# Attention products as 64x32 tiles, with the order of the second pass's steps changed

## The reference, cut to what matters

```python
Q = query @ Wq + bq            # 32 query heads, 4 groups on each of 8 key/value heads, 16 wide
K = key @ Wk + bk
V = value @ Wv + bv
scores = einsum('bhgqd,bhkd->bhgqk', Q, K) * scale
w = softmax(scores, axis=-1)
y = einsum('bhgqk,bhkd->bhgqd', w, V)
x = x + y @ Wo + bo
...
logits = x_n @ gate_w;  routing_weights = top_k(logits, 2)
shared_out = (relu(x_n @ up_w) ** 2) @ down_w
routed_out = (x_n @ fc1_w @ expert_w * sum(routing_weights)) @ fc2_w
x = x + layernorm(shared_out + routed_out, gamma, beta)
```

## Time and profile before

| what | us |
|---|---|
| median of 3 runs (685.68 to 687.26) | 686.53 |
| the profiled execution | 687.42 |
| its span in the profile | 685.6 |
| second pass from its turn -1 to the end | 245.7 to 685.6 |

### The profile page before, as it was taken

How to read it: one execution, slowest core, us unless ns; L and a number is a source line. 1 busy time by engine, 2 the same in 40 slices (tenths; PEclk the granted TensorE clock), 3 DMA queues, 4 the chain that set the end, 5 groups by cost and what they waited for, 6 DMA issues and landing times.

```text
span 685.6 us, 12653 instructions
## 1 busy us (share of the span) xinstructions
PE 654.6 (95%) x3964; PEld 482.3 (70%) x3964; DVE 511.4 (75%) x1140; ACT 432.0 (63%) x793; POOL 378.5 (55%) x464
## 2 busy tenths in 40 slices
PE   7889999999999898999999999999999999998986
PEld 3455666666656476788778787887878878786775
DVE  4999998999975877777677677776777767775444
ACT  4788888888746785574655846658367474674221
POOL 1388999888775534435455354554454545535351
PEclk9999999999999999999999999999999999999999
DMA  8334434352126321121212312113021221211000
GB/s 269 121 109 124 139 123 124 123 180 98 62 94 173 117 79 33 46 64 61 63 35 57 90 33 61 45 49 90 31 61 54 69 61 31 61 31 47 17 16 31
DMA packets 32551, 54.37 MB, mean 79 GB/s; under 512 B 5344, under 2 KB 7136, under 8 KB 32512
## 3 DMA queue, kind: packets, MB, share of 16 engines
q1 hardware_dynamic: 32512, 53.90, 26.6%
HBM read 36.84 MB, written 8.39 MB: 66 GB/s over the span
## 4 chain that ended last, share of the span: by engine, by line
PE 78%; DVE 11%; issue 4%; DMA 3%; ACT 3%; POOL 1%; SPq 0%; POOLq 0%; DVEq 0%; ACTq 0%
PE ps_b L1295 8%; PE ps_b L1297 7%; PE ps_b L1296 7%; PE wide L1295 7%; PE wide L1297 6%; PE wide L1296 6%; PE ps_b L1496 4%; PE ps_a L1340 4%; PE bank L1432 3%; DMA ctx_t<-in_ctx 3%; PE wide L1422 3%; PE ps_b L1350 3%; PE ps_a L1295 2%; PE ps_a L1297 2%; PE wide L1550 2%
## 5 line engine op out<-in xcount | busy, mean ns | idle before, releaser
L780 POOL TENSOR_TENSOR va<-mv,small 128x1 f32<-128x1 f32 x80 | 15.3, 192 | 149.0 <-DVE mv L1274 79.5
L745 ACT ACTIVATE stage<-wide 128x512 f32<-128x512 f32 x30 | 16.3, 595 | 83.8 <-PE bank L1597 83.7
L868 POOL TENSOR_TENSOR y_l<-y,y_h 128x512 fp32r<-128x512 f32 x16 | 21.9, 1370 | 72.5 <-ACT y_h L653 72.5
L1142 DVE RECIPROCAL y<-ps_b 128x256 f32<-128x256 f32 x32 | 55.9, 1748 | 0.4 <-PE ps_b L1496 0.4
L676 ACT ACTIVATE probs<-wide 128x1024 f32<-128x1024 f32 x32 | 32.8, 1025 | 36.1 <-PE wide L1550 36.1
L1295 PE MATMUL wide<-up_h,t_h 128*128 128x512 f32 x128 | 52.1, 407 | 1.5 <-DVE t_l L1226 1.5
L1297 PE MATMUL wide<-up_h,t_l 128*128 128x512 f32 x128 | 50.9, 398 | 0.0
L1296 PE MATMUL wide<-up_l,t_h 128*128 128x512 f32 x128 | 50.4, 394 | 0.0
L1295 PE MATMUL ps_b<-down_h,ht_h 128*128 128x512 f32 x120 | 49.6, 413 | 0.4 <-DVE ht_l L1214 0.4
L782 POOL TENSOR_TENSOR rs<-va,small 128x1 f32<-128x1 f32 x80 | 44.5, 557 | 6.3
L1297 PE MATMUL ps_b<-down_h,ht_l 128*128 128x512 f32 x120 | 47.2, 393 | 0.0
(11 more groups left out here) (244 smaller groups left out, 2155.9 us busy)
## 6 DMA issues: line engine op xcount, KB each, us to landing
q_stack<-qt_h SPq DMA_DIRECT2D x128, 64.0 KB, 2.0
ctx_t<-in_ctx SPq DMA_DIRECT2D x16, 256.0 KB, 2.7
x_res<-in_x SPq DMA_DIRECT2D x16, 256.0 KB, 2.9
x_in<-x_rows SPq DMA_DIRECT2D x16, 256.0 KB, 2.7
ctx_t<-in_ctx_turned SPq DMA_DIRECT2D x16, 256.0 KB, 2.9
x_res<-x_rows SPq DMA_DIRECT2D x16, 256.0 KB, 2.9
out<-stage SPq DMA_DIRECT2D x15, 256.0 KB, 3.0
x_in<-in_x SPq DMA_DIRECT2D x8, 256.0 KB, 3.0
```

The lines of the kernel that those rows point to most:

```text
L1142: dve.reciprocal(y[:, :, b, :], part[:, 1]).then_inc(S["den_s"], 1)
```

## The change

Tiles 0 and 1 keep the old products (`apart(t)`, `APART = 2`). From tile 2 on:

- `vbd` is filled with ones outside its diagonal blocks (once, at tile 2), so the tile of one head and one batch is 64 rows by 32 columns: 16 of values and 16 of ones. `attend` makes 16 products of 64x32 where it made 16 of 128x32: head h of a pair sits in rows 64h on and writes bank 2+h. The numerators of head 0 and the denominators of head 1 of a pair then stand in the wrong halves for each other: in bank 2 rows 0 to 15 of a pair's 32 are numerators and rows 16 to 31 denominators, in bank 3 it is the other way round.
- ACT copies both banks out (`attended_out`: two copies `sums`, then a third of bank 2, scaled by a 0/1 column into `y`). SP moves the denominators to their rows with eight DMAs of 16 rows (`denominators`), ahead of `stacked`. DVE adds the masked numerators of bank 3 (`numerators`), takes two reciprocals in SBUF (`inverted`) and multiplies once (`attended`).
- `output` does its eight products with `y_h` before it waits for `y_l`, then the four with `y_l`.
- Steps are moved on each engine. On PE: `turned_hidden(i, 0)` ahead of `turned_queries`; the routed upper half behind `down(i, 0)`; `output` behind `down(i, 1)`; `turned_norm` and `turned_maxima` behind `output`; both `scores` ahead of `queries`, with `products_kv` between them. On ACT: `y_high`, `query_high` and `guard_rows` follow one another behind `queries_stacked`; both `weights_of` ahead of the routed copies. On DVE and POOL as the diff shows.

```diff
-            def attend(t):
+            def attend_ready(t):
                 if live(t):
                     pe.wait_ge(S["vbd_s"], t + 1)
                     wait(pe, S["kv_s"], capped(1, t + 2))
                     wait(pe, S["z_s"], t - 2)
+                    pe.wait_ge(S["probs_s"], 2 * t + 2)
+            def attend(t):
+                if apart(t):
...
+                elif live(t):
+                    for b in range(2):
+                        for p in range(PAIRS):
+                            for h in range(2):
+                                k = slice(SEQ * h, SEQ * (h + 1))
+                                last = pe.matmul(bank[2 + h][STACK * p:STACK * (p + 1), HALF * b:HALF * (b + 1)],
+                                                 vbd[k, b, p].rearrange("k h d -> k (h d)"), probs[k, b, p, :],
+                                                 start=True, stop=True)
                         last.then_inc(S["pv_ps"], 1)
...
             def output(t):
                 if live(t):
+                    pe.wait_ge(S["y_hi"], t + 1)
+                    for g in range(GROUPS):
+                        pe.matmul(bank[2], cols(y_h, g, P), cols(wo_h, g, D), start=(g == 0), stop=False)
+                        pe.matmul(bank[2], cols(y_h, g, P), cols(wo_l, g, D), start=False, stop=False)
                     pe.wait_ge(S["y_lo"], t + 1)
                     for g in range(GROUPS):
-                        last = split_product(bank[2], cols(y_h, g, P), cols(y_l, g, P),
-                                             cols(wo_h, g, D), cols(wo_l, g, D), g == 0, g == GROUPS - 1)
+                        last = pe.matmul(bank[2], cols(y_l, g, P), cols(wo_h, g, D), start=False, stop=(g == GROUPS - 1))
                     last.then_inc(S["wo_ps"], 1)
...
+            def denominators(t):
+                if live(t) and not apart(t):
+                    sp.wait_ge(S["sums_s"], 2 * (t - APART) + 1)
+                    wait(sp, S["wo_ps"], t)
+                    for h in range(2):
+                        for p in range(PAIRS):
+                            at, beside = STACK * p + HD * h, STACK * p + HD * (1 - h)
+                            sp.dma_start(den[at:at + HD], sums[h][beside:beside + HD]).then_inc(S["den_in"], 16)
...
             def body2(i):
                 load2(i + 4)
-                stacked(i + 3)
                 residual(i + 2)
+                denominators(i + 2)
...
+                stacked(i + 3)
...
+            def attended_out(t):
+                if live(t) and not apart(t):
+                    act.wait_ge(S["pv_ps"], 2 * t + 2)
+                    act.wait_ge(S["qy_ps"], capped(1, t + 2))
+                    for h in range(2):
+                        last = act.activation(sums[h][:].rearrange("p g b q -> p b g q"),
+                                              bank[2 + h].rearrange("p (b g q) -> p b g q", b=2, g=GROUPS), ACT.Copy)
+                    last.then_inc(S["sums_s"], 1)
+                    wait(act, S["wo_ps"], t)
+                    act.activation(y[:].rearrange("p g b q -> p b g q"),
+                                   bank[2].rearrange("p (b g q) -> p b g q", b=2, g=GROUPS), ACT.Copy, scale=place[0]
+                                   ).then_inc(S["sums_s"], 1)
...
+                elif live(t):
+                    dve.wait_ge(S["sums_s"], 2 * (t - APART) + 2)
+                    dve.scalar_tensor_tensor(y[:], sums[1][:], place[1], y[:], ALU.mult, ALU.add).then_inc(S["den_s"], 1)
+            def inverted(t, b):
+                if live(t) and not apart(t):
+                    dve.wait_ge(S["den_in"], DEN_MOVES * (t - APART + 1))
+                    dve.reciprocal(den[:, :, b, :], den[:, :, b, :]).then_inc(S["den_s"], 1)
```

More of the change, by code:

```diff
@@ L157, in build @@
         x_in, ctx_t = sb("x_in", [P, D]), sb("ctx_t", [P, D])
+        with ExitStack() as tmp:
+            sums = [sb(f"sums{h}", [P, GROUPS, 2, SEQ], stack=tmp) for h in range(2)]
         x_h, x_l = sb("x_h", [P, D], F32R), sb("x_l", [P, D], F32R)
@@ L284, in build, with apart, folded @@
         LEAD2 = 4
+        APART = 2
+        def apart(t):
+            return isinstance(t, int) and t < APART
+        def folded(n, tiles):
+            return n * (min(max(tiles, 0), NT - APART) if isinstance(tiles, int) else tiles)
         MOVES = 16 * 2 * PAIRS
+        DEN_MOVES = 16 * 2 * PAIRS
         EARLY = NT - 2
@@ L750, in body2 @@
                     hidden_high(NT - 1, 0)
+                queries_stacked(i + 3)
+                y_high(i + 2)
+                query_high(i + 4)
                 if opening(i):
-                    guard_rows(2)
-                    query_high(3)
                     down_high(1)
-                else:
-                    query_high(i + 4)
-                    guard_rows(i + 3)
+                guard_rows(i + 3)
                 weights_of(i + 3, 0)
+                weights_of(i + 3, 1)
                 t = i + 1
@@ L1233, in body2 @@
                     hidden_low(t, 0)
+                keys_low(i + 3)
+                queries_low(i + 3)
+                numerators(i + 2)
+                context_low(i + 4)
+                normalised(i + 4)
+                maxima(i + 3, 0)
+                inverted(i + 2, 0)
+                t = i
+                if live(t) and not final(t):
+                    hidden_low(t, 1)
+                inverted(i + 2, 1)
                 attended(i + 2)
-                if opening(i):
-                    down_low(0)
+                maxima(i + 3, 1)
                 t = i + 1
@@ L1243, in body2 @@
                     dve.tensor_tensor(rw[:], lg[:, 0:1], lg[:, 1:2], ALU.add).then_inc(S["rw_s"], 1)
-                maxima(i + 3, 0)
-                context_low(i + 4)
-                if isinstance(i, int) and i < 0:
-                    third(i + 2)
-                    normalised(i + 4)
-                else:
-                    normalised(i + 4)
-                    third(i + 2)
-                maxima(i + 3, 1)
-                t = i
-                if live(t) and not final(t):
-                    hidden_low(t, 1)
                 if closing(i):
@@ L1258, in body2 @@
                     hidden_low(NT - 1, 1)
-                third_norm(i + 2)
+                if opening(i):
+                    down_low(0)
                 values(i + 3)
-                keys_values(i + 4)
+                third(i + 2)
+                norm_low(i + 4)
                 if opening(i):
@@ L1594, in turned_hidden @@
                 if not final(t):
+                    wait(pe, S["ht_lo"], 2 * t + part)
                     wait(pe, S["qx_lo"], capped(1, t + 4))
@@ L1640, in body2 @@
                 if live(t) and not final(t):
-                    wait(pe, S["y_s"], capped(2, t + 3))
+                    turned_hidden(t, 1)
+                    wait(pe, S["sums_s"], folded(2, t + 3 - APART))
                     down(t, 0)
-                output(i + 2)
-                t = i
-                if live(t) and not final(t):
-                    turned_hidden(t, 1)
-                rough_scores(i + 3, 1)
                 t = i + 1
                 if live(t):
-                    wait(pe, S["x3_s"], capped(1, t + 2))
-                    routed_part(t, 0, HALF, bank[2][:, HALF:])
-                if opening(i):
-                    turned_maxima(2)
-                    keys_values(3)
-                else:
-                    keys_values(i + 4)
-                    turned_maxima(i + 3)
+                    routed_part(t, HALF, D + EXPERTS, bank[4])
+                rough_scores(i + 3, 1)
                 if closing(i):
@@ L1662, in body2 @@
                     down(t, 1)
+                output(i + 2)
+                turned_norm(i + 4)
+                turned_maxima(i + 3)
+                t = i + 1
+                if live(t):
+                    wait(pe, S["x3_s"], capped(1, t + 2))
+                    routed_part(t, 0, HALF, bank[2][:, HALF:])
                 if closing(i):
@@ L1667, in body2 @@
                 scores(i + 3, 0)
+                products_kv(i + 4)
+                scores(i + 3, 1)
                 queries(i + 4)
-                scores(i + 3, 1)
             pass2_loop(pe, body2, turn_one, turn_two)
```

66 lines of the change are left out of this document (41 added, 25 removed).

## The result

The changed kernel takes 702.01 us (median of 6 runs, 700.85 to 708.30) against 685.69 us before (6 runs, 685.54 to 687.26): ratio 1.0249, 95% interval 1.0216 to 1.0282. It is slower, as forecast, but by 16.3 us where the prediction had 7.1, and outside the range by a hair (its upper end was 702.0).

What follows compares the result with a forecast made beforehand. PE, busy 95% of the span, was taken as the bound. Turns 0 to 11 at +0.26 each (+3.1), opening +2.0 and last turns +2.0 gave +7.1 on 687.42, so 694.5, median 693.6 us; range 682 to 702.

Steps and rivals of the forecast that it cites:

- The attention products: `attend` on PE: the 64x32 products run eight at once, 0.86 us instead of 1.72, gaining 0.86 a tile.
- Rival B: `attend` on PE: row halves don't run eight at once, so it stays at 1.72 us; 705.6 us, chance 0.08.
- The scores' wait: PE's first scores wait for ACT's guard rows, 0.97 us a turn; E is the end of `output`.
- The wait at `output`: PE waits 0.15 us a turn for `y_high` behind DVE's second reciprocal; T is the turn's start.
- Rival C: The denominators' moves come late, at T+12.0, and `output` slips by 0.8 us a turn; 704.8 us, chance 0.12.
- Opening turn: Maxima behind both reciprocals and a norm, `down_low(0)` ahead of the routed half's sum: +2.0 us, bounds 0 and 3.5.
- Last turns: Turn 13 +1.5 us, waiting for the last tile's norm; turn 12 +0.8; turn 14 gives back 0.3: +2.0.
- A: ACT's copies do not hold the scores, a full turn is -0.71 us; 682.0 us, faster, chance 0.18.
- D: Half of the ends' and scores' cost: scores' wait 0.6 us, ends +2; 687.2 us, same, chance 0.08.
- The range: 682 to 702 us, said to leave out Rival B, most of Rival C and A's lower half, together 0.2.

Runs made afterwards that it cites:

- f_mended_old: f_mended with the old attention products in every tile, no copies of sums and no moves of denominators: 697.14 us, ratio 1.0159.
- e_maxima_inside: The changed kernel with `guard_rows` ahead of `query_high` on ACT and the maxima turned inside `output` on PE: 694.35 us, ratio 1.0121.
- e_bias_late: The changed kernel with POOL's residual bias sum moved behind the squares: 698.25 us, ratio 1.0184.
- f_last: f_mended with old products for the last tile, its output ahead of `down(13, 1)`, its norm ahead of tile 13's sum: 686.11 us, ratio 0.9988.
- e_old_products: The changed kernel's new order with the old attention products in every tile, no sums copies or denominator moves: 709.78 us, ratio 1.0349.
- f_mended: f_both with the opening's first maxima and wait for weights moved, and turn 12's routed copies between the two exponentials: 686.16 us, ratio 0.9988.
- g_all: f_mended with `y_high`, `y_low` and the down-weight split moved in the opening, and turn 13's third norm ahead of tile 13's sum: 683.62 us, ratio 0.9956.
- h_final: g_all with the opening's both maxima ahead of `normalised` and the key/value bias sum ahead of the second down-weight split: 684.25 us, ratio 0.9966.
- f_both: The changed kernel with the edits of e_maxima_inside and e_bias_late together: 687.07 us, ratio 1.0012.

## Why the prediction was wrong

- **The attention products, -0.86 a tile.** Right: 1.87 became 1.02. Eight 64x32 products do run at once, 32 records in about 0.87 (1.02 less the hand-over of 0.15), 27 ns each, and f_mended_old gives 0.80 a turn for them. Rival B is out.
- **The scores' wait, +0.97.** Right in place, cause and size: 0.89 at the matmul, and E to the scores 3.53 (411.04 to 414.57) where 3.41 was written.
- **The wait at `output`, +0.15. This is the step that failed.** It rested on the sentence that the first reciprocal may start as late as T+11.2 and on durations of DVE's steps taken from a turn in which POOL's bias sum stood elsewhere. The change moves that sum beside `context_low`, and the STT of y is new beside POOL's products. Both run slower for it, 1.78 and 1.11 instead of 0.68 and 0.75 (the latter in turn 13 of e_maxima_inside, at 643.95), and the first reciprocal comes at T+11.95. Cost up to E: `down(i, 1)` starts about 0.36 late (402.83 to 405.09 is 2.26, against 1.57 of routed work and 0.33 of rough product), `output` starts 3.05 behind it for 2.84, and takes 2.90 for 2.80: 0.67 in all, where 0.15 was forecast. The turn was to grow by 0.26 and grew by 0.93; of the missing 0.67 this step is 0.52 and the chain from E to the scores 0.12. e_bias_late takes 0.57 back by undoing this one step. Nor were the denominators late: the moves end at 399.86, and land 1.9 later (part 6), a microsecond ahead of the reciprocal. Only in turns 12 and 13 does DVE wait for them (0.93 and 4.98 us), and f_last, without the moves of the last tile, was not faster. Rival C had the right place and the wrong cause.
- **Opening turn, +2.0.** Measured +5.3. The larger part is the clock, which the prediction put at nothing. e_old_products shows it: tile 1 has the old products in both kernels, so PE's work in this turn is the same. PE after, then in e_old_products:

```profile
264.67 0.85 PE L1385 MATMUL bank<-small,x_in 128*128 128x128 f32 x4
```

```profile
258.49 0.39 PE L1591 MATMUL ps_a<-kbd_b,qt_b 64*128 64x256 bf16 x4 [2.45 <-DVE gmax L1164]
...
261.71 0.60 PE L1385 MATMUL bank<-small,x_in 128*128 128x128 f32 x4
```

  Both kernels come out of the wait for the maxima (2.46 and 2.45) 14.26 us into the turn. From there to the turned queries it is 5.82 us after, at half clock (the `output` stretch 5.28 instead of 2.8), and 3.22 in e_old_products, which has 1.00 in all of 255 to 270; its opening turn is 28.03, +2.4. So some 2.9 of the 5.3 is the clock in the profiled execution, and what is left is near the forecast. Of that, the wait for the maxima was foreseen; that the scores wait in this turn too, and longer, since `down_high(1)` (1.90 us) also stands ahead of the guard rows, was not.
- **Last turns, +2.0.** Measured +3.3: turn 12 +1.0 (0.8 forecast), turn 13 +2.7 (1.5 forecast), the rest -0.4 (-0.3). Turn 13's excess has 0.7 from the clock, by f_mended.
- **Ahead of the opening turn** nothing was forecast and the profile has -1.2. The new kernels with the same first pass start their opening turn between 243.8 and 248.2, so this is spread between executions.
- **Rivals A and D.** A (no scores' wait, 682) described what was to be had rather than what the change did: with the order mended the kernel is at 683.6. D (687.2) had the scores' wait at 0.6 and the ends at 2, which measured 0.89 and 8.6.
- **The range.** The bounds given for the forecast, a scores' wait of 0.6 to 1.3 and ends of +2 to +8, give +0.7 and +15.1, so 687.2 to 701.6 and not 688.5 to 700; the lower end is rival D itself. B, most of C and half of A have together about 0.25, not 0.2.

The forecast of the sign was right for the main reason given. In the profile the size fell short by 7.3 us in the turns, 3.3 in the opening and 1.3 at the end, less the 1.2 ahead.

## What to carry to other kernels

When a step moves onto an engine's timeline beside another engine's work, take its price from a row where the two stand side by side, not from where they stand alone; a slack of 0.3 us (maxima done at T+10.9, reciprocal allowed at T+11.2) does not survive a step that grows by 1.1. If a change puts a producer late on purpose, bring the whole chain behind it forward in the same edit: here moving one step on ACT and one on PE was worth 7.5 us. And look at the turns that enter and leave the steady state one by one, since they cost nearly half of the whole loss (8.6 of 17.8 us), and their waits can drop the clock.

## What was not expected of the hardware

VectorE and GpSimd slow each other, at times by much more than the two pieces of work add up to. VectorE operations went from 0.68 to 1.78 (`c_l`), from 0.54 to 4.67 (a norm beside three GpSimd operations in a row), and a sum of one element per partition from 0.16 (g_all, 260.59) to 1.70 (f_mended, 261.95). GpSimd loses too: 3.38 for 1.28 beside a 2.28 us split. Near `c_l` the ends lie as if the operations had gone one after another: the sum of y ends at 396.59, GpSimd's bias sum at 397.75, `c_l` at 398.29. The norm is another case: it started ahead of the second and third GpSimd operation and ended behind both, while in after's opening (255.43) it took 2.16 and ended behind the first of three; why, stays open. Not everything is slowed: the maxima, which read PSUM, took 1.29 beside GpSimd's k_stack and y_l (h_final, 255.86) as anywhere, and the reciprocal, which reads one SBUF tile, 1.74 beside the squares (402.76 after).

The granted clock fell to half behind waits of PE of 1.9 to 3.3 us in most kernels that had one: behind the 1.94 us at turn 13's start in all six, in the opening turn in all but e_old_products and f_both, which waited 2.45 and 2.46 us at the same place and have 1.00 in every stretch there. It also fell behind shorter ones: in f_last behind 1.11 and 0.66 us (0.76 in 630 to 635), in f_mended_old behind 1.45 at turn 14's start (0.66 in 665 to 670), where f_mended waited 1.46 and kept 1.00. So a wait makes the drop possible and not certain, in these single executions, and what decides it stays open. What it costs shows between executions of one kernel: after took 700.85 us with a granted clock of 0.997 over the run, 705.16 with 0.989 and 708.30 with 0.982.
